# Moving the second layer normalisation from the node stage (ScalarE) into the expert loop (VectorE, on gathered rows)

## The reference, cut to what matters

```python
x = x + gnn(layernorm(x), W1, b1, W2, b2, edges)      # mean over the in-edges of a node
n = layernorm(x)                                      # (x - mean) / sqrt(var + 1e-5)
mu, var = mean(n), mean((n - mu) ** 2)                # the experts normalise once more
xn = (n - mu) * rsqrt(var + 1e-5) * gamma + beta
w, e = softmax(top_k(xn @ Wr + br, 2))
x = x + sum(w * (gelu(xn @ W1[e] + b1[e]) @ W2[e] + b2[e]))   # over the 2 chosen experts
```

## Time and profile before

| what | us |
|---|---|
| median of 3 runs | 1127.35 |
| lowest and highest | 1125.36 and 1128.64 |
| span of the profiled execution, first to last instruction | 902.9 |
| the median less the span (start and end of the program) | 224.45 |
| busy PE, PEld, DVE, ACT, POOL | 834.7, 652.2, 651.0, 628.3, 602.4 |

### The profile page before, as it was taken

The page is one execution under the profiler, slowest core; times in us unless marked ns, Lnnn a source line. Parts: engine busy times, 40 slices in busy tenths (PEclk is TensorE's granted clock), DMA queues, the critical chain, the costliest instruction groups (busy, mean ns, idle before and its releaser), DMA issues. The chain is left out here.

```text
span 902.9 us, 17755 instructions
## 1 busy us (share of the span) xinstructions
PE 834.7 (92%) x4088; PEld 652.2 (72%) x4089; DVE 651.0 (72%) x1764; ACT 628.3 (70%) x1393; POOL 602.4 (67%) x615
## 2 busy tenths in 40 slices
PE   6997999999999989989999999989999999999997
PEld 3444767767676666766666666768888999999996
DVE  6846888888888888878888887756894455455443
ACT  4425788888888888888898889845554555555553
POOL 2317777777777777777777777659404677776764
PEclk9998999999999999999999999999999999999999
DMA  8547777878888778888887878819852344444443
GB/s 255 171 150 220 247 239 245 247 234 251 240 243 236 247 231 243 241 238 238 245 248 235 230 233 264 228 49 281 265 139 54 59 73 75 81 71 68 76 71 45
DMA packets 91000, 169.47 MB, mean 188 GB/s; under 512 B 17604, under 2 KB 56910, under 8 KB 90840
## 3 DMA queue, kind: packets, MB, share of 16 engines
q0 software_dynamic: 43696, 122.35, 49.8%
q1 hardware_dynamic: 46232, 44.79, 17.0%
q10 hardware_dynamic: 944, 0.92, 0.4%
HBM read 146.98 MB, written 21.43 MB: 187 GB/s over the span
## 5 line engine op out<-in xcount | busy, mean ns | idle before, releaser
L1001 POOL DMA_INDIRECT gath<-q_rows,idx_t x408 | 391.9, 960 | 138.8 <-issue 93.3
L1068 DVE SCALAR_TENSOR_TENSOR h_lo<-bank,h_hi 128x512 fp32r<-128x512 f32 x327 | 219.4, 682 | 40.1 <-ACT h_hi L1250 38.0
L1250 ACT ACTIVATE h_hi<-bank 128x512 fp32r<-128x512 f32 x327 | 191.0, 598 | 45.5 <-DVE bank L1063 20.9
L1231 ACT ACTIVATE bank<-gath 128x512 f32<-128x512 f32 x287 | 173.4, 604 | 14.3 <-DMA gath<-q_rows,idx_t 10.5
L1384 PE MATMUL bank<-p_hi,ohT 128*128 x287 | 123.4, 430 | 42.8 <-ACT bank L1231 40.3
L1428 PE MATMUL agg_ps<-h_hi,oh 128*128 128x512 f32 x408 | 161.9, 397 | 0.3 <-DVE h_lo L1068 0.2
L1429 PE MATMUL agg_ps<-h_lo,oh 128*128 128x512 f32 x408 | 161.3, 395 | 0.0
L1995 POOL DMA_INDIRECT out<-y_out,sca_i x56 | 93.7, 1673 | 49.0 <-issue 15.9
L1384 PEld LDWEIGHTS bank<-p_hi,ohT 128*128 128x128 f32 x287 | 54.1, 189 | 91.2 <-issue 83.0
L1385 PE MATMUL bank<-p_lo,ohT 128*128 x287 | 113.9, 397 | 0.0
L2099 PE MATMUL bank<-tokT,fw_now 128*128 128x128 f32 x896 | 109.3, 275 | 0.8 <-ACT tokT L2055 0.8
(11 more groups left out here) (287 smaller groups left out, 1276.6 us busy)
## 6 DMA issues: line engine op xcount, KB each, us to landing
rows_sb<-rel_blocks SPq DMA_DIRECT2D x102, 128.0 KB, 4.3
fw<-in_L_ffn_W SPq DMA_DIRECT2D x16, 512.0 KB, 5.1
gath<-q_rows,idx_t POOLq DMA_INDIRECT x408, 4.4
q_rows<-q_buf SPq DMA_DIRECT2D x25, 256.0 KB, 2.4
out<-x_all SPq DMA_DIRECT2D x28, 128.0 KB, 3.8
x_all<-in_x SPq DMA_DIRECT2D x25, 128.0 KB, 2.7
xm_rows<-xt SPq DMA_DIRECT2D x25, 128.0 KB, 3.0
x_all<-in_x SPq DMA_DIRECT2D x2, 640.0 KB, 10.3
```

The costliest lines, as they stand in the source:

```text
L1001: pool.indirect_dma_start(out=gath[:, j % RING, :], out_offset=None, in_=q_rows[:, :], in_offset=bass.IndirectOffsetOnAxis(ap=idx_t[:, j:j ...
L1068: dve.scalar_tensor_tensor(out=h_lo[:, j % LO_RING, :], in0=z_of(slot0, j), scalar=0.0, in1=h_hi[:, j % HI_RING, :].bitcast(F32), op0=ALU. ...
L1231: actv.activation(z_of(slot0, j), gath[:, j % RING, :], ACT.Copy).then_inc(s_seed, 1)
L1250: actv.activation(h_hi[:, j % HI_RING, :], z_of(slot0, j), ACT.Relu).then_inc(s_hi, 1)
```

## The change

- `xm_rows` now gets `x_all` itself, un-normalised. `xt`, its ring of four buffers, and `normalise` on ScalarE are gone.
- The inverse root and the negated mean times that root are no longer made tile by tile. ScalarE takes the roots in three groups (10, 8 and 7 tiles), VectorE inverts and negates them within the routing steps, of which there are 17 in place of 16, and they travel as tags 4 and 5 of each row (TAGS 4 to 6; a row of `xm_rows` grows from 1040 to 1048 bytes).
- In the FFN VectorE normalises the gathered rows in place before TensorE transposes them: one `tensor_scalar` of 128x256 for each of the 56 slots, three slots ahead; slots 0, 1 and 2 come before the loop.
- Three expressions that give semaphore values mask their register (`tile & 31`, `cur & 31`, `turn & 1023`); the values stay the same.

```diff
-TAGS = 4
+TAGS = 6
+        rstd2, nmr2 = tags[:, :, 4], tags[:, :, 5]
@@ edge stage, ScalarE and TensorE @@
-                        actv.wait_ge(s_evac, cur * 2 + (CREDIT + 1))
+                        actv.wait_ge(s_evac, (cur & 31) * 2 + (CREDIT + 1))
-                    pe.wait_ge(s_evac, tile * 2 + (CREDIT - 2))
+                    pe.wait_ge(s_evac, (tile & 31) * 2 + (CREDIT - 2))
@@ node stage, SyncE @@
                     sp.wait_ge(s_x1, t + 1)
+                    sp.dma_start(xm_rows[t * P:(t + 1) * P, 0:D], x_all[:, t, :]).then_inc(s_xm_st, 16)
                     sp.dma_start(out[t * P:(t + 1) * P, :], x_all[:, t, :]).then_inc(s_x1_st, 16)
-                    if t:
-                        store_xt(t - 1)
@@ node stage, VectorE @@
                     if n == 3:
-                        dve.wait_ge(s_rstd, t1)
+                        dve.wait_ge(s_std2, ROOTS.index(t1) + 1)
+                        then(dve.reciprocal(rstd2[:, part], std2[:, part]))
+                    if n == 4:
                         then(dve.tensor_tensor(logit[:, part, :], logit[:, part, :], rstd2[:, part].unsqueeze(2).to_broadcast(shape), ALU.mult))
-                    if n == 4:
+                    if n == 5:
+                        then(dve.scalar_tensor_tensor(out=nmr2[:, part], in0=mv2[:, part, 0], scalar=-1.0, in1=rstd2[:, part],
+                                                      op0=ALU.mult, op1=ALU.mult))
-                LOGIT_STEPS = 5
+                LOGIT_STEPS = 6
-                    if 0 <= i - 1 < NT:
-                        invert(i - 1)
-                    if 0 <= i - 1 < NT:
-                        negate(i - 1)
@@ node stage, ScalarE @@
-                    if 0 <= i - 2 < NT:
-                        root(i - 2)
-                    if 0 <= i - 2 < NT:
-                        normalise(i - 2)
+                    if i - 1 in ROOTS:
+                        root(max([0, *(t for t in ROOTS if t < i - 1)]), i - 1)
@@ FFN, GpSimd @@
-                            pool.wait_ge(s_put[(i - back) % PUTS], turn[back - 1][i])
+                            pool.wait_ge(s_put[(i - back) % PUTS], turn[back - 1][i] & 1023)
@@ FFN, VectorE @@
+                def normalise(i):
+                    dve.wait_ge(s_tok[i % TOK], 16 * (i // TOK + 1))
+                    rows, tag = tok[:, i % TOK, 0:D], tok[:, i % TOK, D:]
+                    dve.tensor_scalar(rows, rows, tag[:, 4:5], tag[:, 5:6], ALU.mult, ALU.add).then_inc(s_tokN, 1)
                 copy_weights(0)
                 copy_weights(1)
+                for i in range(3):
+                    normalise(i)
                 weigh(0)
                 weigh(1)
                 for i in range(MS):
                     if i + 2 < MS:
                         copy_weights(i + 2)
+                    if i + 3 < MS:
+                        normalise(i + 3)
@@ FFN, TensorE @@
                 def turn_tok(i):
-                    pe.wait_ge(s_tok[i % TOK], 16 * (i // TOK + 1))
+                    pe.wait_ge(s_tokN, i + 1)
```

More of the change, by code:

```diff
@@ L45 @@
 FIRST_RING, FIRST_ADDED_AHEAD, FIRST_SEEDED_AHEAD, FIRST_SEED_AHEAD = 5, 5, 4, 8
-XT_RING = 4
 def is_added(j):
@@ L273, in build @@
         std2 = sb("std2", [P, NT], F32, c_ctx)
-        rstd2 = sb("rstd2", [P, NT], F32, c_ctx)
-        nmr2 = sb("nmr2", [P, NT], F32, c_ctx)
         aggT = sb("aggT", [P, 2, H], F32, c_ctx)
         bias_in = sb("bias_in", [P, 2, D], F32, c_ctx)
-        xt = sb("xt", [P, XT_RING, D], F32, c_ctx)
         spare = agg_all[:, :, :].rearrange("p t h -> p (t h)")
@@ L1261, in close @@
                         if last:
-                            actv.wait_ge(s_evac, cur * 2 + (CREDIT + 2))
+                            actv.wait_ge(s_evac, (cur & 31) * 2 + (CREDIT + 2))
                             settle(actv)
                             return
-                        actv.wait_ge(s_evac, cur * 2 + (CREDIT + 1))
+                        actv.wait_ge(s_evac, (cur & 31) * 2 + (CREDIT + 1))
                         settle(actv)
@@ L1552, in build @@
         s_std2 = sem("s_std2")
[L1553 to L1556, removed]
         s_x1_st = sem("s_x1_st")
+        s_xm_st = sem("s_xm_st")
         s_logit = sem("s_logit")
@@ L1572, in build @@
         TOK, FIRST_TOK = 6, 2
+        PART1, PART2 = 10, 18
+        ROOTS = [PART1, PART2, NT]
         s_tok = [sem(f"s_tok{b}") for b in range(TOK)]
@@ L1585, in store_x1 @@
                     sp.wait_ge(s_x1, t + 1)
+                    sp.dma_start(xm_rows[t * P:(t + 1) * P, 0:D], x_all[:, t, :]).then_inc(s_xm_st, 16)
                     sp.dma_start(out[t * P:(t + 1) * P, :], x_all[:, t, :]).then_inc(s_x1_st, 16)
-                def store_xt(t):
-                    sp.wait_ge(s_xt, t + 1)
-                    sp.dma_start(xm_rows[t * P:(t + 1) * P, 0:D], xt[:, t % XT_RING, :]).then_inc(s_xt_st[t % XT_RING], 16)
                 def load_expert(e):
@@ L1597, in _ @@
                     store_x1(t)
-                    if t:
-                        store_xt(t - 1)
                     if t % 3 == 2 and t // 3 < NEXP:
                         load_expert(t // 3)
-                store_xt(NT - 1)
                 sp.dma_start(b1_rows[:], f_b1.rearrange("e (k p) -> (e k) p", p=P)).then_inc(s_bias, 16)
@@ L1611, in _ @@
                 sp.wait_ge(s_x1_st, 16 * (NT + 3))
-                for k in range(XT_RING):
-                    sp.wait_ge(s_xt_st[k], 16 * len(range(k, NT, XT_RING)))
+                sp.wait_ge(s_xm_st, 16 * NT)
                 sp.wait_ge(s_fw, 32 * NEXP)
@@ L1658, in variance @@
                     dve.bn_aggr(mv2[:, t, :], stats2[:, t, :]).then_inc(s_var, 1)
[L1660 to L1667, removed]
                 def finish_logits(n, t0, t1):
@@ L1724, in _ @@
                 then(dve.memset(earlier[:, 0:1, 0:1], 0.0))
-                LOGIT_STEPS = 5
+                LOGIT_STEPS = 6
                 STEPS = LOGIT_STEPS + 11
-                PART1, PART2 = 10, 18
                 for i in range(NT + 1):
@@ L1864, in _ @@
                         pool.tensor_tensor(x_all[:, t - 1, :], x_all[:, t - 1, :], bias_in[:, (t - 1) % 2, :], ALU.add).then_inc(s_res, 1)
-                for k in range(XT_RING):
-                    pool.wait_ge(s_xt_st[k], 16 * len(range(k, NT, XT_RING)))
+                pool.wait_ge(s_xm_st, 16 * NT)
                 pool.wait_ge(s_tags, 16)
@@ L1877, in copy_aggT, with root @@
                     actv.activation(aggT[:, t % 2, :], bank[t % 2][:], ACT.Copy).then_inc(s_aggT, 1)
[L1879 to L1887, removed]
+                def root(t0, t1):
+                    actv.wait_ge(s_var, t1)
+                    actv.activation(std2[:, t0:t1], mv2[:, t0:t1, 1], ACT.Sqrt, bias=eps2_col[:], scale=1.0 + EPS).then_inc(s_std2, 1)
                 for i in range(NT + 2):
@@ L1947, in build @@
         OUTS, BATCH8, PUTS = 5, 8, 3
+        s_tokN = sem("s_tokN")
         s_tokT_ps = sem("s_tokT_ps")
```

## The result

The changed kernel takes 1130.88 us (median of 20 runs, 1129.19 to 1136.57), the kernel before in the same comparison 1128.89 us (20 runs, 1123.95 to 1131.39). The ratio is 1.0031, 95% interval 1.0020 to 1.0041: slower by about 3.5 us, where the forecast was 0.6 us faster and no measurable change. The ratio is formed from all the runs; the two medians lie only 2.0 us apart, so the size is uncertain by a microsecond or two and the direction isn't.

The account below looks back on a forecast made before the run. GpSimd's queue was taken to bound the edge stage, TensorE the node stage, routing and FFN. Terms -1.9 (node stage), +1.1 (first slot), +0.2 (slots with loads) gave -0.6 us: 1127.35 to 1126.8 us, range 1123.5 to 1131.

Parts of the forecast that it names:

- the masks': Edge stage: one more register operation of about 42 ns before each of 408 aggregations, hidden; 0, at most 0.5 us.
- The pace of the gathers: Edge stage: GpSimd's queue sets the pace, 408 gathers starting over 514.8 us, 1.265 us each.
- the masks, or the tight slots, in the open: Rival: a third of 17 us of masks, or 0.4 us at a dozen slots, exposed; 1131 to 1133 us, chance 0.05.
- Node stage: ScalarE's copy `aggT` no longer waits behind VectorE, removing TensorE's idle time: 1.9 us gained, bounds 1.0 and 2.0.
- FFN start: First transposes wait for slot 0's normalisation, queued behind two weight copies: 1.1 us lost, bounds 0.9 and 1.6.
- The slots with loads: FFN loop: six slots where VectorE loads expert numbers first leave little room for the normalisation: 0.2 us, bounds 0 and 1.2.
- The rival in which GpSimd falls behind: FFN: VectorE's operations hold up GpSimd's scatters until TensorE waits; worst case some 5 us, 1132 us, chance 0.08.
- 0.37 us for a scatter that is held up: FFN: a VectorE operation that blocks GpSimd's scatter adds up to 0.37 us (1.96 in place of 1.59).
- A: Theory of the follow-up experiments, not the prediction: the masks cost time through TensorE's extra register operation in every edge-stage slot.
- C: Theory of the follow-up experiments, not the prediction: the loss is the FFN start.
- the same 224.45 us around it: Last step: profile span 902.9 to 902.3 us, plus an unchanged 224.45 us, takes the time from 1127.35 to 1126.75.
- The prediction's own range: Whole kernel: 1124.5 to 1130 us, from the sum's bounds and the runs' scatter of 1.3 to 2 us.

Follow-up runs that it names:

- e9: Kernel before with only the register masks added, on a chip where the kernel before takes 903.64 us: 906.38 us, ratio 1.0027.
- e8: Kernel before with the masks and one product of zero weights, 256 columns, behind each aggregation: 923.57 us, ratio 1.0214.
- e12: Kernel before with the masks, TensorE's taken twice, on a chip where the kernel before takes 903.64 us: 909.45 us, ratio 1.0066.
- e1: Kernel before with only the register masks added, on a chip where the kernel before takes 1108.3 us: 1111.03 us, ratio 1.0026.
- e3: Kernel before with the masks, TensorE's taken twice, on a chip where the kernel before takes 1108.3 us: 1113.87 us, ratio 1.0044.
- e2: The whole change, unaltered, on a chip where the kernel before takes 1108.3 us: 1112.39 us, ratio 1.0026 to the kernel before.
- e10: The whole change, unaltered, on a chip where the kernel before takes 903.64 us: 904.74 us, ratio 1.0010 to the kernel before.
- e16: The whole change, unaltered, on a chip where the kernel before takes 903.39 us: 904.68 us, ratio 1.0016 to the kernel before.

## Why the prediction was wrong

**The step that failed** is the masks': "I take 0, with 0.5 as the upper bound for the last few slots", because the operation "lies under the products before it, and behind GpSimd's pace". It measures 2.7 us. The pace of the gathers was read rightly: 408 in 514.4 us after (66.1 to 580.5, e9). But from GpSimd's short waits the prediction concluded that "nothing that TensorE or ScalarE does a little later changes the pace", and e8 shows that more work of TensorE does; and it took the stage's pace for its end. The end is the last aggregation: 12 of the 408 start behind the last gather, over 12 us, and TensorE, with 465 of 514 us busy, has little room. The bound should have come from that load: a part of 408 x 36 ns, between 0 and 14.7 us. The rival "the masks, or the tight slots, in the open", with 1131 to 1133 us, was the nearest; it had a chance of 0.05, and its price, "a third of 17 us", was twice too high. That the operations in TensorE's queue cost this much is shown (e9, e12, e1, e3); what each slot makes of the 36 ns, and why a fifth reaches the end, is only argued from the waits.

**Node stage**: -1.9 forecast, 2.2 us gained (56.4 us, and 54.2 or 54.3 in all ten profiles of the change). Right, a little more than the upper bound of 2.0; no wait for `aggT` is left but the first.

**FFN start**: +1.1 forecast, 0.9 at the least. The transposes came 1.02 us later and the first product 0.8: right in mechanism, a little high in size. The normalisation took 0.41 us (0.36 each for the two in a row), not 0.35. The remaining 1.8 us of the chips at over 1,100 us, in two profiles of the whole change, the prediction didn't have. The same mark stands in a pause of e2's edge stage, where ScalarE waits for TensorE's result:

```profile
415.27 0.60 ACT L1247 ACTIVATE h_hi<-deg_ps 128x512 fp32r<-128x512 f32 x1 [2.66 <-remote]
```

So the late result may be one more of the interruptions that the last section shows; that isn't shown.

**FFN loop**: the first to the last product of the second layer take 204.5 or 204.6 us in every profile, before and after (691.8 to 896.4 before). The slots with loads cost nothing that shows; 0.2 was forecast. The rival in which GpSimd falls behind didn't happen. Its scatters in e10, and one of them beside the copy and the normalisation:

```profile
L1966 POOL DMA_INDIRECT out<-y_out,sca_i x56: 1552/1589/2102, 694.0 to 897.4; - x56
...
713.22 1.59 POOL L1966 DMA_INDIRECT out<-y_out,sca_i  x1 [1.65 <-DVE w_now L1999]
713.45 0.69 DVE L1989 COPY fw_now<-fw 128x1024 f32 x1 [0.61 <-PE bank L2079]
714.06 0.41 DVE L1994 TENSOR_SCALAR agg_all<-agg_all 128x256 f32<-128x256 f32 x1
```

Their mean is 1.645 us, before 1.673. Here both of VectorE's operations lie inside the scatter, and it takes the median. So an operation that begins behind the start of a scatter need not hold it up. One that begins just ahead does, in the kernel before:

```profile
814.92 0.69 DVE L2018 COPY fw_now<-fw 128x1024 f32 x1
814.97 2.10 POOL L1995 DMA_INDIRECT out<-y_out,sca_i  x1 [0.57 <-DVE w_now L2023]
```

Six of the 56 scatters before have a copy that began 0.05 to 0.11 us ahead, and take 2.04 to 2.10 us; in e10 four have one, 0.05 to 0.14 us ahead, and take 2.01 to 2.10. The prediction's 0.37 us for a scatter that is held up should thus have been 0.5. By the rule from the Trainium skill (SBUF — State Buffer, "Who interferes with whom") the operation that starts first keeps the other out; for such copies the trace agrees. For the normalisation no row shows it: e10's scatter at 721.19 us starts within one (720.88 to 721.29) and takes 1.59 us.

**Sum by the measured terms**: on a quick chip 2.7 - 2.2 + 0.8 = +1.3 us, where e10 and e16 measured medians 1.1 and 1.3 us over the kernel before. On the other kind 2.7 - 2.2 + 0.8 + 1.8 = +3.1 us, where e2 has 1.0026 of 1108.3, 2.9 us (4.1 between the medians), and the result 1.0031 of 1128.9, 3.5 us (2.0 between the medians). The agreement is within that scatter and no closer. A is the largest term; what C names is 0.8 us, and 2.6 on the other kind.

**Around the span**: "with the same 224.45 us around it" was wrong as a reading: these are a longer edge stage on another chip. It cost the sum little, since the terms carry over, but it hid that the clock that the rows were read at (1.00, in the edge stage 0.99) wasn't that of the timed runs, 0.90 in the mean of each. The prediction's own range, 1124.5 to 1130, takes the runs' scatter in at its lower end only: 1127.35 + 2.3 + 1.3 would be 1131.

Left open: what stretches the edge stage on some chips, and why the first FFN results come late there only in the whole change. No version was found that is measurably faster than the kernel before. The test that is missing is the change without TensorE's masks, whose wait takes the same values without them: by the measured terms it would lie 1.4 us below the kernel before on a quick chip, and 2.2 us with the first normalisation ahead of the copies (estimates).

## What to carry to other kernels

The engine with the steadiest interval seems to pace a stage, but the stage ends with its last consumer. A small addition to another engine's stream isn't free because the pacer hardly waits: look at that engine's busy share (here 465 of 514 us) and at how far behind the pacer it ends, and run a variant in which the addition is doubled. A register operation that repeats in each of several hundred slots is a term of the sum, even at 36 ns. Where the span and the time of the runs differ by more than a few us, find out first in which stage; a profile from another chip has other waits.

## What the runs showed of the hardware

The kernel before took 903.4 to 903.9 us on three chips, 1108.3 on a fourth and 1128.9 in the comparison of the result; in the profiles the difference is all in the edge stage. Three neighbouring stretches of e2, two of 5 us and one of 2 us, columns as in the earlier trace rows:

```profile
395.00:400.00 5.00, 5.00 (x21) 3.48 (x20) 2.10 (x6) 1.93 (x5) 3.80 (x4) 1.00 0.84 242
400.00:405.00 5.00, 1.79 (x6) 1.38 (x6) 2.95 (x8) 3.21 (x7) 0.39 (x1) 0.87 0.32 96
405.00:407.00 2.00, 2.00 (x6) 1.51 (x6) 1.87 (x4) 1.32 (x3) 1.51 (x2) 0.50 0.69 170
```

At full clock TensorE works. Then its weight loads stand for 3.6 us, and the idle times before the other engines start again are 3.9 us (ScalarE), 4.3 (VectorE) and 4.8 (GpSimd); when TensorE goes on the granted clock falls to 0.50, that is 1.2 in place of 2.4 GHz. This pause and the next two end 14 us apart:

```profile
403.24 0.19 PEld L1381 LDWEIGHTS deg_ps<-p_hi,ohT 128*128 128x128 f32 x1 [3.64 <-issue]
...
417.42 0.29 PEld L1381 LDWEIGHTS bank<-p_hi,ohT 128*128 128x128 f32 x1 [3.29 <-issue]
...
431.23 0.29 PEld L1381 LDWEIGHTS bank<-p_hi,ohT 128*128 128x128 f32 x1 [3.68 <-issue]
```

In the profile of 1129.0 us the node stage and the FFN, with TensorE 59.33 of 60 and 209.17 of 217 us busy and transfers at 229 and 68 GB/s, run at clock 1.00 and lose nothing but the 1.8 us at the FFN start. What tells the edge stage from them for the chip no run here shows.
